# Stream norms as a pipeline over eight units, and an MLP with two output banks

## The reference, cut to what matters

```python
def _ln(x):                                     # over the 128 channels
    mu = jnp.mean(x, axis=-1, keepdims=True)
    var = jnp.var(x, axis=-1, keepdims=True)
    return (x - mu) * jax.lax.rsqrt(var + EPS)
...
# layers 1 and 2, the MLP at their end
xm = _ln(x) * (1.0 + sc_ff) + sh_ff
h = jax.nn.gelu(xm @ fc1_w + fc1_b, approximate=True)     # 128 -> 512
x = x + g_ff * (h @ fc2_w + fc2_b)                        # 512 -> 128
...
# last layer, its start
nx = _layer_norm(x, ln_gamma, ln_beta)
q = nx @ Wq
k = prototype_bank @ Wk
scores = jnp.einsum('bth,bph->btp', q, k) * H ** (-0.5)
```

## Time and profile before

| what | us |
|---|---|
| median of three runs (6663.01 to 6669.19) | 6666.6 |
| the profiled execution | 6661.25 |
| its span in the trace | 6659.4 |
| m1, from the first L439 to the end of the last L502 | 105.9 |
| m2, the same | 106.5 |
| l3's norm part, from the first L559 to the end of the last L789 | 46.6 |

### The profile page before, as it was taken

How to read it: one execution, slowest core, us unless ns; L and a number is a source line. 1 busy time by engine, 2 the same in 40 slices (tenths; PEclk the granted TensorE clock), 3 DMA queues, 4 the chain that set the end, 5 groups by cost and what they waited for, 6 DMA issues and landing times.

```text
span 6659.4 us, 147906 instructions
## 1 busy us (share of the span) xinstructions
PE 6053.3 (91%) x49714; PEld 3131.7 (47%) x49714; DVE 4120.8 (62%) x6520; ACT 4244.6 (64%) x8158; POOL 985.0 (15%) x1660
## 2 busy tenths in 40 slices
PE   6999999999777999999999677799999999979998
PEld 3444444444444444444444344344444444435554
DVE  5777767766555676666775355577776777634333
ACT  3777777777665777777776466477777777732222
...
GB/s 86 76 66 59 71 71 60 65 77 43 54 57 78 69 64 66 78 72 70 59 75 34 25 58 58 60 76 66 59 71 77 60 59 78 34 33 42 43 46 22
DMA packets 180929, 402.17 MB, mean 60 GB/s; under 512 B 16992, under 2 KB 124560, under 8 KB 166416
## 3 DMA queue, kind: packets, MB, share of 16 engines
...
## 4 chain that ended last, share of the span: by engine, by line
PE 73%; DVE 8%; issue 8%; ACT 7%; DMA 2%; SPq 1%; POOL 1%; ACTq 0%; DVEq 0%; POOLq 0%
PE bank L1062 18%; PE bank L1108 18%; PE pair L1078 14%; DVE MX L1404 3%; PE bank L1034 2%; ACT P L1238 2%; PE bank L649 2%; PE bank L1029 2%; PE bank L640 2%; DMA QP<-scr_q 2%; PE pair L1095 1%; PE pair L1084 1%; ACT QP L1249 1%; PE pair L578 1%; DVE ST L1361 1%
## 5 line engine op out<-in xcount | busy, mean ns | idle before, releaser
L1238 ACT ACTIVATE P<-bank 128x512 f32<-128x512 f32 (+1 forms) x5504 | 3103.6, 597 | 1350.2 <-PE bank L1062 1302.1
L1404 DVE TENSOR_REDUCE MX<-pair 128x2 f32<-128x802 f32 x3072 | 2922.7, 988 | 1297.6 <-PE pair L1078 1289.0
L1062 PE MATMUL bank<-QP,KP 128*128 128x256 bf16 (+1 forms) x11008 | 2089.9, 276 | 143.9 <-ACT P L1238 91.1
L1108 PE MATMUL bank<-P,VA 128*25 128x256 f32 (+1 forms) x22016 | 1755.6, 391 | 6.1 <-issue 0.7
L1078 PE MATMUL pair<-KP,QP 96*128 96x401 bf16 x6144 | 1574.6, 338 | 62.2 <-DMA QP<-scr_q 42.3
L1062 PEld LDWEIGHTS bank<-QP,KP 128*128 128x128 bf16 (+1 forms) x11008 | 857.5, 100 | 1578.2 <-ACT P L1238 915.1
L1108 PEld LDWEIGHTS bank<-P,VA 128*25 128x25 f32 (+1 forms) x22016 | 401.9, 102 | 711.2 <-issue 456.7
L1078 PEld LDWEIGHTS pair<-KP,QP 96*128 96x128 bf16 x6144 | 593.1, 98 | 182.2 <-DVE MX L1404 64.8
L1529 POOL COPY VA<-VN 128x416 f32<-128x416 f32 (+1 forms) x320 | 140.0, 438 | 2517.6 <-PE bank L1108 2436.4
L1408 DVE TENSOR_REDUCE MX<-pair 128x4 f32<-128x1024 f32 x256 | 311.1, 1222 | 324.5 <-PE pair L1084 324.0
L1249 ACT CAST QP<-pair 2x512 bf16<-2x512 f32 x640 | 339.4, 576 | 128.7 <-PE pair L1095 123.1
...
## 6 DMA issues: line engine op xcount, KB each, us to landing
...
KP<-scr_ks SPq DMA_DIRECT2D x128, 144.0 KB
...
```

The costliest lines, as they stand in the source:

```text
L1062: last = nc.tensor.matmul(SC[half][0:kt, k * N:(k + 1) * N], KP[g][:, c0:c0 + kt], QP[g][:, h * N:(h + 1) * N], start=True, stop=True)
L1108: last = nc.tensor.matmul(OB[32 * h:32 * h + STEP + HD + 1, 0:N], VA[g % 2][0:kt, t, h, :], P[(g * ph.nt + t) % 2][0:kt, h * N:(h + 1) * N ...
L1238: nc.scalar.activation(P[v % 2][0:kt, half * 2 * N:(half + 1) * 2 * N], SC[half][0:kt, :], ACT.Exp, scale=SCALE).then_inc(sem("probs_full" ...
L1404: nc.vector.tensor_reduce(MX[:, r, c:c + 2], MP[j % 2][:, :].rearrange("p (t k) -> p t k", t=2)[:, :, 0:SPANS[0][1]], AX.X, ALU.max).then_ ...
```

## The change

The loops of the norm part and of the MLP part in m1 and m2, and of l3's norm part, are written out with constant addresses. The norm runs over eight units with four buffer sets (`SETS`, XCU and SQU, taken in turn; unit, Ln and Exp are done in place), and each engine's program is staggered: in m1 and m2 TensorE issues the mean of unit u and then the variance of u-2, ScalarE the square of u and then Ln and Exp of u-2, VectorE the center of u and then unit and modulation of u-3. In l3 it is mean u, variance u-1, l_q u-2, l_k u-3; square u, Ln and Exp u-1, copy u-2; center u, unit and gamma u-1, QKA copy u-4. Means, variances and projections use two banks in turn, with waits that a bank has been read. In the MLP part the outputs go to banks 6 and 7 in turn (both are free in m1 and m2), gated into XC and SQ in turn; L450's successor waits only for the norm of its own unit (the first one also for the last Ln, which frees banks 2 and 3), and the wait for mlp_gated of two units ago stands ahead of the second group of products. Some semaphores no longer start at 1.

```diff
--- before.py
+++ after.py
-        self.c0 = Count(dict(l_centered=1), norms, B // 2)
+        self.c0 = Count({}, norms, B // 2)
...
-    start = dict(probs_full=3, pv_done=2, heads_copied=2, mlp_centered=1, mlp_gated=1)
+    start = dict(probs_full=3, pv_done=2, heads_copied=2)
...
-        XCS, SQS = [XC[:, :], P[0][:, 0:2 * N]], [SQ[:, :], P[0][:, 2 * N:4 * N]]
-        LGS, RSTDS = [LG[:, :], P[1][:, 0:2 * N]], [RSTD[:, :], P[1][:, 2 * N:4 * N]]
-        XNS, XMS = [XN[:, :], REST[:, 0:2 * N]], [XM[:, :], REST[:, 2 * N:4 * N]]
-
+        SETS = 4
+        XCU = [XC[:, :], LG[:, :], XN[:, :], REST[:, 0:2 * N]]
+        SQU = [SQ[:, :], RSTD[:, :], XM[:, :], REST[:, 2 * N:4 * N]]
+        XMS = [P[0][:, 0:2 * N], P[0][:, 2 * N:4 * N]]
+        GATED = [XC[:, :], SQ[:, :]]
+        def unit(src, u):
+            return src[:, u * 2 * N:(u + 1) * 2 * N]
...
+            def mean(u):
+                if u >= 2:
+                    pe.wait_ge(sem("mlp_centered"), at("mlp_centered", u - 2, 1))
+                nc.tensor.matmul(bank[u % 2][:, :], w("mean"), unit(X, u), start=True, stop=True).then_inc(
+                    sem("mlp_mean"), 1)
+            def var(u):
+                pe.wait_ge(sem("mlp_squared"), at("mlp_squared", u, 1))
+                if u >= 2:
+                    pe.wait_ge(sem("mlp_log"), at("mlp_log", u - 2, 1))
+                nc.tensor.matmul(bank[2 + u % 2][:, :], w("mean"), SQU[u % SETS], start=True, stop=True).then_inc(
+                    sem("mlp_var"), 1)
+            for u in range(B // 2 + 2):
+                if u < B // 2:
+                    mean(u)
+                if u >= 2:
+                    var(u - 2)
+            for i in range(B // 2):
+                if i == 0:
+                    pe.wait_ge(sem("mlp_log"), at("mlp_log", B // 2 - 1, 1))
+                pe.wait_ge(sem("mlp_normed"), at("mlp_normed", i, 1))
                 for c in range(4):
-                    if c == 0:
-                        pe.wait_ge(sem("mlp_gated"), at("mlp_gated", i, 0))
-                    nc.tensor.matmul(bank[2 + c][:, :], w(ph.name + "w1", c * D, D), XMA[:, ds(i * 2 * N, 2 * N)],
+                    nc.tensor.matmul(bank[2 + c][:, :], w(ph.name + "w1", c * D, D), unit(XMA, i),
                                      start=True, stop=True).then_inc(sem("mlp_hidden"), 1)
+                if i >= 2:
+                    pe.wait_ge(sem("mlp_gated"), at("mlp_gated", i - 2, 1))
                 for c in range(4):
                     pe.wait_ge(sem("mlp_act"), at("mlp_act", i, c + 1))
-                    last = nc.tensor.matmul(bank[6][:, :], w(ph.name + "w2", c * D, D), HM[c], start=(c == 0),
+                    last = nc.tensor.matmul(bank[6 + i % 2][:, :], w(ph.name + "w2", c * D, D), HM[c], start=(c == 0),
                                             stop=(c == 3))
                 last.then_inc(sem("mlp_out"), 1)
...
+            def square(u):
+                act.wait_ge(sem("mlp_centered"), at("mlp_centered", u, 1))
+                if u >= SETS:
+                    act.wait_ge(sem("mlp_unit"), at("mlp_unit", u - SETS, 1))
+                nc.scalar.activation(SQU[u % SETS], XCU[u % SETS], ACT.Square).then_inc(sem("mlp_squared"), 1)
+            def root(u):
+                act.wait_ge(sem("mlp_var"), at("mlp_var", u, 1))
+                nc.scalar.activation(SQU[u % SETS], bank[2 + u % 2][:, :], ACT.Ln, bias=w("eps6")).then_inc(
+                    sem("mlp_log"), 1)
+                act.wait_ge(sem("mlp_log"), at("mlp_log", u, 1))
+                nc.scalar.activation(SQU[u % SETS], SQU[u % SETS], ACT.Exp, scale=-0.5).then_inc(sem("mlp_rstd"), 1)
+            for u in range(B // 2 + 2):
+                if u < B // 2:
+                    square(u)
+                if u >= 2:
+                    root(u - 2)
             nc.scalar.preload_act_table(ACT.Gelu_apprx_tanh)
-            with loop(act, 0, B // 2) as i:
+            for i in range(B // 2):
...
+            def center(u):
+                if u >= SETS:
+                    dve.wait_ge(sem("mlp_normed"), at("mlp_normed", u - SETS, 1))
+                dve.wait_ge(sem("mlp_mean"), at("mlp_mean", u, 1))
+                nc.vector.tensor_tensor(XCU[u % SETS], unit(X, u), bank[u % 2][:, :], ALU.subtract).then_inc(
+                    sem("mlp_centered"), 1)
+            def norm(u):
+                dve.wait_ge(sem("mlp_rstd"), at("mlp_rstd", u, 1))
+                nc.vector.tensor_tensor(XCU[u % SETS], XCU[u % SETS], SQU[u % SETS], ALU.mult).then_inc(
+                    sem("mlp_unit"), 1)
+                dve.wait_ge(sem("mlp_unit"), at("mlp_unit", u, 1))
+                for r in range(2):
+                    b = 2 * u + r
+                    last = nc.vector.tensor_scalar(XMA[:, b * N:(b + 1) * N], XCU[u % SETS][:, r * N:(r + 1) * N],
+                                                   modcol(ph.mod[0], b), modcol(ph.mod[1], b), ALU.mult, ALU.add)
+                last.then_inc(sem("mlp_normed"), 1)
+            for u in range(B // 2 + 3):
+                if u < B // 2:
+                    center(u)
+                if u >= 3:
+                    norm(u - 3)
+            dve.wait_ge(sem("mlp_normed"), at("mlp_normed", B // 2 - 1, 1))
+            for i in range(B // 2):
+                if i >= 2:
+                    dve.wait_ge(sem("stream_done"), at("stream_done", i - 2, 1))
                 dve.wait_ge(sem("mlp_out"), at("mlp_out", i, 1))
                 for r in range(2):
-                    last = nc.vector.tensor_scalar(XC[:, r * N:(r + 1) * N], bank[6][:, r * N:(r + 1) * N],
+                    last = nc.vector.tensor_scalar(GATED[i % 2][:, r * N:(r + 1) * N],
+                                                   bank[6 + i % 2][:, r * N:(r + 1) * N],
                                                    w(ph.name + "b2"), modcol(ph.gate, i * 2 + r), ALU.add, ALU.mult)
                 last.then_inc(sem("mlp_gated"), 1)
                 dve.wait_ge(sem("mlp_gated"), at("mlp_gated", i, 1))
-                nc.vector.tensor_tensor(X[:, ds(i * 2 * N, 2 * N)], X[:, ds(i * 2 * N, 2 * N)], XC[:, :],
-                                        ALU.add).then_inc(sem("stream_done"), 1)
-                dve.wait_ge(sem("stream_done"), at("stream_done", i, 1))
+                nc.vector.tensor_tensor(unit(X, i), unit(X, i), GATED[i % 2], ALU.add).then_inc(sem("stream_done"), 1)
+            dve.wait_ge(sem("stream_done"), at("stream_done", B // 2 - 1, 1))
...
+            at0 = ph.c0.at
+            def mean(u):
+                if u >= 2:
+                    pe.wait_ge(sem("l_centered"), at0("l_centered", u - 2, 1))
+                nc.tensor.matmul(bank[u % 2][:, :], w("mean"), unit(X, u), start=True, stop=True).then_inc(
+                    sem("l_mean"), 1)
+            def project(u, name, need, free, first, lhsT, rhs):
+                pe.wait_ge(sem(need), at0(need, u, 1))
+                if u >= 2:
+                    pe.wait_ge(sem(free), at0(free, u - 2, 1))
+                nc.tensor.matmul(bank[first + u % 2][:, :], lhsT, rhs, start=True, stop=True).then_inc(sem(name), 1)
+            def norms():
+                for u in range(B // 2 + 3):
+                    if u < B // 2:
+                        mean(u)
+                    if 1 <= u < B // 2 + 1:
+                        project(u - 1, "l_var", "l_squared", "l_log", 2, w("mean"), SQU[(u - 1) % SETS])
+                    if 2 <= u < B // 2 + 2:
+                        project(u - 2, "l_q", "l_normed", "l_qf", 4, w3c("wq"), unit(XMA, u - 2))
+                    if u >= 3:
+                        project(u - 3, "l_k", "l_qf", "l_qk", 6, w3c("wkT"), XMS[(u - 3) % 2])
...
+            def norms():
+                for u in range(B // 2 + 3):
+                    if u < B // 2:
+                        if u >= SETS:
+                            act.wait_ge(sem("l_unit"), at0("l_unit", u - SETS, 1))
+                        one(at0, u, "l_squared", "l_centered", 1, SQU[u % SETS], XCU[u % SETS], ACT.Square)
+                    if 1 <= u < B // 2 + 1:
+                        sq = SQU[(u - 1) % SETS]
+                        one(at0, u - 1, "l_log", "l_var", 1, sq, bank[2 + (u - 1) % 2][:, :], ACT.Ln, bias=w("eps5"))
+                        one(at0, u - 1, "l_rstd", "l_log", 1, sq, sq, ACT.Exp, scale=-0.5)
+                    if 2 <= u < B // 2 + 2:
+                        if u >= 4:
+                            act.wait_ge(sem("l_k"), at0("l_k", u - 4, 1))
+                        one(at0, u - 2, "l_qf", "l_q", 1, XMS[u % 2], bank[4 + u % 2][:, :], ACT.Copy)
...
+            def norms():
+                for u in range(B // 2 + 4):
+                    if u < B // 2:
+                        if u >= SETS:
+                            dve.wait_ge(sem("l_normed"), at0("l_normed", u - SETS, 1))
+                        dve.wait_ge(sem("l_mean"), at0("l_mean", u, 1))
```

(18 more changed lines are left out.)

88 lines of the change are left out of this document (5 added, 83 removed).

## The result

The changed kernel takes 6588.8 us (median of four runs, 6586.2 to 6591.6). The kernel before, run beside it, takes 6664.8 (6655.5 to 6669.2). The ratio is 0.9888, with an interval of 0.9871 to 0.9905: 76 us or 1.1% faster. The direction was right, but the forecast of 6606 and its range from 6597 up were too slow: it missed by 17.5 us. The profiled execution took 6589.53 us with a span of 6587.6.

The account below looks back on a forecast made before the run. TensorE, busy 91% of the span, bounds the kernel, but the changed parts are held by chains and waits. Gains of 25.9 (m1), 26.5 (m2) and 7.9 (l3), together 60.3, taken from 6666.6 give 6606 us, range 6597 to 6622.

Parts of the forecast that it names:

- the anchor: The time the gain is subtracted from: the median 6666.6 us, 5.35 above the profiled execution's 6661.25.
- the price of VectorE's waits on itself: Norm part, m1 and m2: a VectorE wait for its own last operation costs 0.13 us, or 0.26.
- Loop entry: Start of the norm parts: the delay before TensorE's first mean goes, gaining 0.7 us in m1 and m2, 0.8 in l3.
- Filling: Norm part, m1 and m2: five products lead to the fourth center, taken to start at 7.9 us.
- The steady cycle: Norm part, m1 and m2: VectorE's center, unit, modulation and waits take 2.29 to 2.55 us a unit, taken as 2.4.
- The end of the norm part: m1 and m2: ScalarE's work behind the eighth center takes 4.5 us, so the first MLP product starts at 22.1.
- MLP part: m1 and m2: units follow without idle at 6.88 us, the last takes 9.1; 58.6 in place of 70.8, gain 12.2 each.
- The first unit's clock: MLP part, m1 and m2: the first unit's loss to half clock is halved from 2.6 to 1.3 us, the wait being shorter.
- Rival 1: The clock stays at half through the norm parts: 23 us lost, 6629, or half of that, 6618; chance 0.12.
- l3: l3's norm part: centers 4.6 us apart, 4.0 at first; 39.5 in place of 46.6, gain 7.1 plus entry 0.8.
- Rival 2: MLP part, m1 and m2: units don't overlap and stay at 8.44 us, 21.8 lost, 6628; chance 0.04.
- Rivals 3 and 4: Half clock through all three parts, 77 us more, 6744, chance 0.02; a later wait takes the gain back, 6666, chance 0.02.

Follow-up runs that it names:

- the deeper stagger: The changed kernel with l3's norm part staggered like m1's (rsqrt multiplication of unit u-3, copy of u-6): 6582.5 us, 7.9 less than the changed kernel beside it.

## Where the prediction was right and where not

The mechanism was right in the main, and the sizes were not. The 17.5 us between 6606.3 and 6588.8 are these: 6.6 in the changed parts, 4.8 outside them in the pair of traces, 5.35 from the anchor, and 0.7 between the changed kernel's profiled execution and its median. Three steps failed: the anchor with the range built on it, all that lies outside the changed parts taken at nothing, and the price of VectorE's waits on itself. The range reached down to 6597. The trace pair's own gain of 71.7 would have given 6594.9 from that anchor, and the medians gained 76.0.

**The anchor and the noise.** I went from the profiled 6661.25 to the median of three, 6666.6. With four, eleven, seven and seven runs the medians were 6664.8, 6660.8, 6662.5 and 6663.2, single runs from 6654 to 6674. A median of three of such runs is uncertain by several us, and I gave it ±3. By the middle of these medians, 6662.9, the same sum gives 6602.6. This step failed on size, and the range with it: it let in too little on the fast side.

**Outside the changed parts** the forecast had nothing. The pair shows 4.8 us: 2 in l3's rest with the pause of VectorE that is gone, the rest from clocks and pieces that move by themselves. "A first pass through new code is no slower" held in the changed kernel's own parts, but not in the variant with the loops alone, whose VectorE paused for 2.10 there.

**Loop entry.** Right: 0.82 fell to 0.06 (3643.78 + 0.48 to 3644.32), 0.76 for the 0.7 taken.

**Filling.** "I take 7.9" for the fourth center: measured 6.47 in m1 and 7.60 in m2. The half clock ended 3.8 us into m1 and 6.1 into m2; in the kernel before it was 6.1 and 3.3, and over all traces of all kernels it is 3.0 to 6.2. So this is a draw of each execution, and "the clock was at half for the first 6 us" was one such draw. Mis-sized by 1.4 and 0.3.

**The steady cycle**, taken as 2.4, was 2.10. The sum 0.61 + 0.69 + 0.13 + 0.73 + 0.13 = 2.29 prices the idle time behind the operation's end from rows of before, where the number waited for or an operand's address was computed from a loop register, and I went up to 2.4 from it. With constants in the code these gaps are 0.04, in the variant with the loops alone too. The fifth to eighth centers come 0.9 us sooner in m1 and 1.2 in m2. By the rule of the Trainium skill, "VectorE: DVE Perf Modes", section "The DRAIN you can't avoid", the prediction had worked out 2.1 for the cycle, and I had gone against it. The trace has 2.10. But the rule's own reason, that the semaphore costs nothing, is not what is measured: with a wait 0.77 pass, without one 0.65.

**The end of the norm part**: 4.6 taken, 4.7 and 4.5 measured (3659.49 to 3664.17, and in m2).

**MLP part.** 6.88 a unit taken, 6.87 measured; 9.1 for the last unit, 8.9 measured. The first unit's clock, "I take half, 1.3", was 2.3 in m1 and 0 in m2. So the parts took 59.2 and 57.0 for 58.6 each: the sum of both is within 1 us, by luck, since the reason given, the length of the gap ahead of the unit, was not the cause (filling it didn't keep the clock). Rival 1's thought, that the clock moves with short idle times, fits this one place; over the whole norm part it did not hold.

**l3.** Centers 4.46 apart for the 4.6 taken, and 3.80 for 4.0 in the first units. VectorE in l3:

```profile
5906.95 0.68 DVE L834 TENSOR_TENSOR LG<-X,bank 128x512 f32<-128x512 f32 x1
5909.62 0.69 DVE L840 TENSOR_TENSOR XC<-XC,SQ 128x512 f32<-128x512 f32 x1 [1.99 <-ACT SQ L742]
5910.35 0.55 DVE L842 TENSOR_SCALAR XMA<-XC,KP 128x512 f32<-128x512 f32 x1
5910.81 0.69 DVE L847 TENSOR_SCALAR W<-bank 128x512 f32<-128x512 f32 x1
5911.41 0.68 DVE L834 TENSOR_TENSOR XN<-X,bank 128x512 f32<-128x512 f32 x1
```

The step L840 to L842 is 0.73, where the earlier trace rows has 0.82: the same 0.09. The idle time of 1.99 for ScalarE is what the deeper stagger takes away. The part took 37.9 for 39.5 taken.

**The rivals.** Rival 2 needs units of 8.4: it is what the run with one bank shows, 19.4 us for the 21.8 priced. Rivals 3 and 4 did not come.
